# A layered token mixer on one core: a new written-out order of steps, and the set-up of the later layers' weights moved behind batch 0's first stage

## What is computed

```python
x = ln(x + rwkv(x))       # time mix: k, v, r = 3 projections to 512; decayed running sums of exp(k), exp(k)*v
                          # over the tokens; sigmoid(r) * wkv / wk @ Wo; then a channel mix (two projections, silu)
x = ln(x + tree_ffn(x))   # gates of 255 tree nodes, leaf probabilities level by level (8 levels), @ leaf values
x = ln(x + attention(x))  # RMS norm, 16 heads of 8 dims, rotary positions, causal softmax
x = ln(x + experts(x))    # 16 experts, softmax routing, top 2; plus 2 shared experts
```

## Time and profile before

| | before |
|---|---|
| median of 3 runs (range) | 1794.94 us (1793.65 to 1797.28) |
| the profiled execution | 1796.05 us, its span 1794.2 us |
| busy share of the span | PE 90%, PEld 60%, DVE 84%, ACT 56%, POOL 49% |
| instructions | PE 12141, DVE 3386, ACT 1998, POOL 1120 |
| chain that ended last, by engine | PE 44%, DVE 38%, issue 5%, POOL 5%, ACT 4% |
| mean granted clock of TensorE | 0.963 of full speed |

### The profile page before, as it was taken

The page is one execution under the profiler, slowest core; times in us unless marked ns, Lnnn a source line. Parts: engine busy times, 40 slices in busy tenths (PEclk is TensorE's granted clock), DMA queues, the critical chain, the costliest instruction groups (busy, mean ns, idle before and its releaser), DMA issues.

```text
span 1794.2 us, 33666 instructions
## 1 busy us (share of the span) xinstructions
PE 1610.9 (90%) x12141; PEld 1076.4 (60%) x12141; DVE 1504.2 (84%) x3386; ACT 1010.6 (56%) x1998; POOL 879.9 (49%) x1120
## 2 busy tenths in 40 slices
...
DMA packets 66921, 53.35 MB, mean 30 GB/s; under 512 B 8322, under 2 KB 65474, under 8 KB 66754
## 3 DMA queue, kind: packets, MB, share of 16 engines
...
q10 hardware_dynamic: 3552, 1.65, 0.3%
...
## 4 chain that ended last, share of the span: by engine, by line
PE 44%; DVE 38%; issue 5%; POOL 5%; ACT 4%; SPq 1%; DMA 1%; DVEq 0%; ACTq 0%; POOLq 0%
PE bank L913 42%; DVE rmax L736 11%; DVE wkb L683 3%; DVE rmax L733 3%; DVE stats L637 3%; DVE prob L816 2%; PE bank L909 2%; DVE inner L646 2%; DVE tree L646 2%; ACT prob L502 1%; DVE mv L642 1%; DVE mixed L646 1%; SPq L333 1%; POOL rstd L359 1%; DVE kvsum L675 1%
## 5 line engine op out<-in xcount | busy, mean ns | idle before, releaser
L502 ACT ACTIVATE prob<-bank 128x512 f32<-128x512 f32 x640 | 355.2, 595 | 107.0 <-PE bank L913 101.9
L736 DVE TENSOR_REDUCE rmax<-bank 128x1 f32<-128x512 f32 (+2 forms) x768 | 352.0, 504 | 11.2 <-PE bank L913 11.0
L447 POOL TENSOR_TENSOR prob<-xdT,spread 128x512 f32<-128x512 f32 x128 | 161.8, 1269 | 244.7 <-ACT spread L502 209.8
L913 PE MATMUL bank<-kh,qh 72*128 72x512 bf16 (+3 forms) x1024 | 260.2, 305 | 19.0 <-DVE rmax L736 13.2
L913 PEld LDWEIGHTS bank<-wexpT,prob 128*128 128x128 f32 x2048 | 259.7, 192 | 19.3 <-issue 14.8
L913 PE MATMUL bank<-wexpT,prob 128*128 128x128 f32 x2048 | 268.5, 277 | 0.0
L913 PE MATMUL bank<-qh,kh 75*128 75x512 bf16 (+3 forms) x1024 | 249.2, 304 | 11.7 <-ACT prob L502 5.6
L502 ACT ACTIVATE spread<-bank 128x512 f32<-128x512 f32 x128 | 76.4, 597 | 249.2 <-PE bank L913 248.3
L683 DVE RECIPROCAL wkb<-wkb 128x512 f32<-128x512 f32 x64 | 211.4, 3323 | 0.0
L913 PEld LDWEIGHTS bank<-qh,kh 75*128 75x128 bf16 x1024 | 100.2, 98 | 171.0 <-ACT prob L502 112.5
L913 PE MATMUL bank<-maskb,identb 128*128 128x128 bf16 x1024 | 191.8, 222 | 0.0
...
## 6 DMA issues: line engine op xcount, KB each, us to landing
...
```

Source lines behind the costliest of these rows:

```text
L447: raised(pool.tensor_tensor(ug[:, e % 4, :], xdT[:, :], spread[e // 2 % 2][:, :], ALU.mult), "ug_side")
L502: raised(act.activation(dst, src, func, **kw), signal)
L736: last = dve.tensor_reduce(rmax[:, j, h:h + 1], S[n % 2][:, col:col + (j + 1) * P], AX_X, ALU.max)
L913: return pe.matmul(out_, w, x, start=start, stop=stop, **kw)
```

## The change

Three edits together.

1. **Loads.** The time mix's five loads (`Wk`, `Wv`, `Wr`, decay, first) get a semaphore of their own, `time_loaded`. ACT issues only three of them besides its small vectors; six loads move from ACT's queue to SP's, where decay and first come first. PE, ACT and DVE wait for `time_loaded` (or the decay made from it) before batch 0's time mix; the wait for all loads goes to the steps that need the weights.
2. **Set-up of the weights.** It becomes a step `weights` that acts for batch 0 alone: on PE behind `read_out3`, on ACT ahead of the next batch's `norm0`, on DVE between `x2` and `moments2`. It uses six banks in turn in place of seven, and the scratch of the shared bias moves from the time mix's tiles to those of the last layers. The bias DMAs become an SP step behind batch 0's second `heads`.
3. **Order.** `ORDER` is replaced on every engine but for the few steps of SP. Most steps keep their neighbours; each engine has some 10 to 50 steps in other places.

```diff
     act="""
-        ... 138:mix_before4 141:norm7 138:cmk_tanh0 138:cmk_tanh1 140:norm6 ...
+        ... 2:mix_before4 2:cmk_tanh0 5:norm7 2:cmk_tanh1 4:norm6 ...
...
+        TIME_LOADS = [(tdec[:, :], a["L0_attn_tm_decay"].rearrange("(c p) -> p c", p=P)), (tfirst[:, :], a["L0_attn_tm_first"].rearrange("(c p) -> p c", p=P)),
+                      (wk[:, :], a["L0_attn_tm_Wk"]), (wv[:, :], a["L0_attn_tm_Wv"]), (wr[:, :], a["L0_attn_tm_Wr"])]
         LOADS = [
-            (wk[:, :], a["L0_attn_tm_Wk"]), (wv[:, :], a["L0_attn_tm_Wv"]), (wr[:, :], a["L0_attn_tm_Wr"]),
             (cwk[:, :], a["L0_attn_cm_Wk"]), (cwr[:, :], a["L0_attn_cm_Wr"]),
...
-            for dst, src in LOADS[ON_ACT:]:
+            for dst, src in TIME_LOADS[0:2]:
+                sp.dma_start(dst, src, allow_slow_non_contiguous=True).then_inc(setup["time_loaded"], 16)
+            for dst, src in LOADS:
                 sp.dma_start(dst, src, allow_slow_non_contiguous=True).then_inc(setup["loaded"], 16)
-            sp.wait_ge(setup["bias_parts"], 7)
-            for i in range(PARTS):
-                sp.dma_start(bias_rows[i:i + 1, :], bias_part[i]).then_inc(setup["bias_in"], 16)
...
-            for dst, src in LOADS[0:ON_ACT]:
-                act.dma_start(dst, src, allow_slow_non_contiguous=True).then_inc(setup["loaded"], 16)
+            for dst, src in TIME_LOADS[2:]:
+                act.dma_start(dst, src, allow_slow_non_contiguous=True).then_inc(setup["time_loaded"], 16)
...
+            def take_weights(b):
+                if b == 0:
+                    take_turns(0, len(TURNS))
...
-            act.wait_ge(setup["loaded"], ALL_LOADED)
+            act.wait_ge(setup["time_loaded"], ALL_TIME)
...
+            def prepare_weights(b):
+                if b == 0:
+                    dve.wait_ge(setup["loaded"], ALL_LOADED)
+                    dve.tensor_scalar(cwv[:, :, :], cwv[:, :, :], 0.5, None, ALU.mult).then_inc(setup["scaled"], 1)
...
+            def turn_weights(b):
+                if b == 0:
+                    pe.wait_ge(setup["loaded"], ALL_LOADED)
+                    for n, (src, rows, _) in enumerate(TURNS):
...
-            pe.wait_ge(setup["loaded"], ALL_LOADED)
+            pe.wait_ge(setup["time_loaded"], ALL_TIME)
             run("pe", pe_steps, BEGUN["pe"])
```

More of the change, by code:

```diff
@@ L51 @@
     sp="""
-        2:heads0 2:heads1 0:load 2:max_rows 4:store
+        2:heads0 2:heads1 1:shared_bias 0:load 2:max_rows 4:store
     """,
     pool="""
-        296:rwkv1 296:r_sig3 296:gated3 297:rope_sum0 296:wk3 297:rest0 296:rwkv2 297:part_lo0 296:rwkv3 297:rope_sum1 297:rest1 295:root0
-        297:part_lo1 296:root2 295:x1_gain 295:x1_bias 296:res 299:root7 295:root1 298:root6 297:root4 296:cmr_sig 296:cmr_sum 298:gate_rest
-        298:gate_lo 298:u1 298:u3 296:root3 298:u5 295:wk0 298:u7 298:u9 298:u11 295:r_sig0 295:gated0 298:u13 298:u15 295:rwkv0 295:wk1 295:r_sig1
@@ L58 @@
-        295:r_sig2 295:wk2 295:gated1 296:root_rms 295:gated2
+        2:part_lo0 1:rwkv3 2:rope_sum1 2:rest1 0:root0 2:part_lo1 1:root2 0:x1_gain 0:x1_bias 2:root4 4:root7 3:root6 1:res 0:root1 1:cmr_sig
+        1:cmr_sum 3:gate_rest 3:gate_lo 3:u1 1:root3 3:u3 3:u5 0:wk0 3:u7 3:u9 3:u11 0:r_sig0 3:u13 3:u15 0:r_sig1 0:gated0 0:rwkv0 0:r_sig2 0:wk1
+        0:wk2 0:gated1 1:root_rms 0:gated2 0:rwkv1 0:r_sig3 0:gated3 1:rope_sum0 0:wk3 1:rest0 0:rwkv2
     """,
     act="""
-        140:exp24 140:exp25 139:part_hi0 140:exp26 140:exp27 140:exp28 139:part_mid0 140:exp29 140:exp30 140:exp31 140:exp32 140:exp33 139:part_hi1
@@ L62 @@
[L62 to L69, removed]
+        2:mix_before4 2:cmk_tanh0 5:norm7 2:cmk_tanh1 4:norm6 2:cmk_tanh2 4:xdT_out 2:cmk_tanh3 4:route_exp 3:values 2:cmr_tanh 1:norm1 3:norm4
@@ L74 @@
[L74 to L81, removed]
+        4:route_probs 3:rowmax10 4:largest0 4:others 3:rowmax11 3:rowmax12 4:largest1 4:gates 3:rowmax13 3:rowmax14 2:y0 3:rowmax15 3:rowmax16 4:u0
@@ new lines @@
+        3:rowmax17 2:moments3 4:u2 3:rowmax18 3:rowmax19 1:mix0 1:mix1 1:mix2 4:u4 3:rowmax20 3:rowmax21 1:clamp0 3:rowmax22 4:u6 3:rowmax23
+        3:rowmax24 1:ksum0 3:rowmax25 3:rowmax26 3:rowmax27 4:u8 3:rowmax28 3:rowmax29 1:kv0 3:rowmax30 3:rowmax31 4:u10 3:rowmax32 3:rowmax33
+        1:kvsum0 3:rowmax34 4:u12 3:rowmax35 1:clamp1 2:tree0 3:rowmax36 1:wkv0 3:rowmax37 3:rowmax38 4:u14 3:rowmax39 2:tree1 3:max_parts 2:tree2
+        2:tree3 1:inverse0 1:kv1 1:clamp2 2:tree4 2:tree5 2:tree6 2:tree7 1:kvsum1 4:yd 1:ksum1 1:wkv1 1:kv2 1:clamp3 1:kvsum2 1:ksum2 1:wkv2 2:yb
@@ L85 @@
[L85 to L96, removed]
```

213 lines of the change are left out of this document (127 added, 86 removed).

## The result

The changed kernel takes 1772.45 us, median of 4 runs (1768.89 to 1774.35), beside 1796.11 for the kernel before in the same runs: a ratio of 0.9867, 95% interval 0.9847 to 0.9888, so 24 us or 1.3% faster. The forecast was 1804.6, the range 1786 to 1810. The profiled execution took 1774.35, its span 1772.6; against 1794.2 that is 21.6 less.

A forecast was written before the change was run, and what follows sets the result against it. The prediction took a loop through DVE (`attend1` to `clamp2`) and PE (from `r2`) as the bound. Per turn 0.45 - 0.60 + 1.45 = +1.30, times 13 = +16.9, less 7.2 at the start: +9.7, median 1804.6 us, range 1786 to 1810.

The forecast's parts named there:

- The bound and the loop: Steady turn of 100.0 us: DVE runs from `attend1` to `clamp2`, then PE from `r2` to the last pair products.
- `r2` waiting for `clamp2` still: Predicted sign in the steady turn: PE's `r2` would still wait for DVE's `clamp2` after the change.
- The start: Up to batch 0's `moments2`: `clamp0` 15.7 us earlier, less 8.5 for the set-up behind `x2`, a gain of 7.2.
- Rival D: Set-up in its new place costs 13 us rather than 8.5, giving 1809; chance 0.08.
- (a): Channel mix: `cmk_tanh0` ahead of `norm7` on ACT makes DVE wait at `silu3`, +0.45 us per turn.
- (b): Row maxima and `tree1` on DVE: small waits +0.38, `tree1` away from POOL's `u11` saves 0.98; together -0.60 us per turn.
- the first part: Row maxima on DVE: waits at `rowmax33` and `clamp1`, one fewer at `rowmax29`, given as +0.38 us per turn.
- (c): `tree3` directly behind `tree2` on DVE meets POOL's `r_sig1` and `gated0` behind `u15`, delaying `clamp2`: +1.45 us per turn.
- (d): The rest of the turn, including `back0` behind `read_out3`, a PE change and shifted scans: 0 us per turn.
- C: `tree3` beside POOL costs nothing because POOL is late with `u15` or `r_sig1`: 1786 us; chance 0.12.
- rival B: `tree3` slips past POOL's `gated0`, costing +0.35 us per turn: 1790 us, faster; chance 0.20.

The follow-up runs named there:

- experiment 6: Changed kernel with `tree1` moved ahead of `rowmax38` on DVE, beside POOL's `u13`: 1782.31 us, ratio 0.9926.
- experiment 7: Changed kernel with `clamp2` moved behind `tree4` and `tree5` on DVE: 1793.31 us, ratio 0.9987.
- experiment 1: Kernel before with the change's loads and set-up but the old order of steps: 1787.49 us, ratio 0.9958.
- experiment 5: Changed kernel with `norm7` again ahead of `cmk_tanh0` on ACT: 1768.80 us, ratio 0.9849.
- experiment 4: Kernel before with `expert 11` alone moved behind `gb15`, `v1` and `r1` on PE: 1787.06 us, ratio 0.9961.
- experiment 3: Changed kernel with `expert 11` and `gb15` again ahead of `v1` and `r1` on PE: 1789.22 us, ratio 0.9966.
- 10: Kernel before with `tree1` alone moved from behind `rowmax34` to between `rowmax39` and `max_parts` on DVE: 1789.34 us, ratio 0.9969.

## Why the prediction was wrong, step by step

**The bound and the loop: right in kind, incomplete.** DVE and PE hand the turn to one another. But the hand-over is not from `clamp2` to `r2` alone: it is also from `u14` to `gb15` (experiment 6) and from `clamp2` over ACT's `k_exp2` to the scores (experiment 7), and these are within some tenths of one another. "`r2` waiting for `clamp2` still" did not hold, and yet the turn followed `clamp2`, by the way over ACT.

**The start: right.** 3.1 at `mixed` was 2.7 (23.32 to 20.63), 15.7 at `clamp0` was 15.0, `x2` at 66.8 was 66.92, the set-up's 8.5 was 7.7, and the 7.2 at `moments2` was 8.14. Alone it is worth 7.5 us (experiment 1). Rival D did not occur.

**(a), 0.45 per turn: too large.** The wait at `silu3` is there and is 0.20, released by ACT as written; undoing the move is worth 0.11 (experiment 5).

**(b), -0.60: right.** 0.30 at `rowmax33`, 0.10 at `clamp1`, one 0.20 fewer, and `tree1` 1.37 to 0.36: -0.8 by these rows. (The terms that the text gives for the first part, 0.4 + 0.24 - 0.2, add up to 0.44 and not to its 0.38; over 13 turns that is 0.8 us.) (a) and (b) together were forecast at -0.15 and came to -0.61 at `max_parts`.

**(c), +1.45: the step that failed.** It came to -0.97, and these 2.4 us per turn are nearly the whole error: 12 to 13 turns of them are 29 to 31 us, and the distance from 1804.6 to 1772.45 is 32. What else differs (in (a), (b) and (d), the start, batches 1 to 3, the last turns) is a few us each and of both signs. The text says that "`tree2` runs beside `u15`" and that "POOL has `r_sig1` and `gated0` directly behind `u15`", and takes for granted that `u15` still starts when `max_parts` ends. `u15` has other waits, one of them for `expert 11`, and PE's part of the same diff moves `expert 11` three steps back. I read the order of DVE and of POOL at that place and not that of PE. Experiment 4 shows the cause with this one step, moved in the kernel before; experiment 3 shows the way back in the changed kernel, with `gb15` moved along. No rival had a gain at this place: C, the lowest, said "(c) costs nothing", and its reason, a late `u15`, was half the truth, but the time given to it left out that `tree2` would be free as well. And the price for `tree3` itself was wrong even where the premise holds: 0.29 in experiment 3, near rival B's 0.35.

**(d), 0: nearly right.** The stretch from `clamp2` to the next `attend1` became 0.30 longer: `x2` is 1.72 earlier in its turn and `attend1` only 1.28, since `back0` now stands behind `read_out3`, as the text has it, without a gain.

**What no step spoke of: the last turns.** From `x2` of batch 15 to the end, the changed kernel takes 5.8 us more. Its clock there, the first and the last of seven windows of 20 us (columns as in the earlier trace rows) that end with the span, of before and then of after:

```profile
1654.00:1674.00 20.00, 13.72 (x94) 9.47 (x95) 15.94 (x51) 7.67 (x19) 3.17 (x8) 0.86 0.24 66
...
1774.00:1794.00 20.00, 11.97 (x96) 11.26 (x96) 4.68 (x13) 4.11 (x9) 7.86 (x9) 0.94 0.05 15
```

```profile
1633.00:1653.00 20.00, 14.55 (x86) 10.05 (x85) 15.26 (x49) 5.73 (x14) 2.12 (x6) 0.72 0.15 43
...
1753.00:1773.00 20.00, 10.60 (x86) 9.85 (x85) 4.00 (x12) 4.04 (x8) 6.58 (x8) 0.88 0.05 14
```

PE idles for a part of these windows, and the granted clock is between its two levels, 1.2 and 2.4 GHz, that is at the lower one for a part of the time. In the seven windows it was 0.86, 0.88, 0.89, 0.94, 0.74, 0.66 and 0.94 before, and 0.72, 0.93, 0.83, 1.00, 0.69, 0.63 and 0.88 after: a mean of 0.84 and 0.81, but two of the seven are higher after. Experiment 3 has the order of the change but for two steps, and its last stretch takes 235.5 us; the changed kernel's takes 240.7. In these two the steps of DVE lie alike, within 0.4, for the first 120 us behind `x2`, and all of the 5 us opens later.

There is a rival to the clock. The four kernels with `expert 11` ahead (before, 1, 3, 10) take 234.9 to 235.9 here, the ten with it behind 237.1 to 240.7. Against it stands one place in experiment 4, which is before but for that step: DVE's steps are alike up to 58.5 us behind `x2`, and the next one (`xb<-xb,bank`), 10.7 later in before, is 12.0 later there. No `expert` lies between the two, and the granted clock is 1.00 in before (window 1617 to 1629) and 0.86 in experiment 4 (1608 to 1620). What of the 5.8 us is the clock and what set it lower stays open: no experiment held it fixed.
